# A fused attention and mixture kernel: the copy of the attention output one unit earlier, and the selection of the fourth query tile moved into the next batch

## What is computed

```python
att = where(causal, q @ k.T / sqrt(8), -inf)
S   = relu(att[:, 0]); S[..., 0] = 0; S = S * (1 - eye)      # head 0
FF  = cumsum(shift_down_by_one(S), axis=query)               # what is forgotten
att = att - FF
rank = argsort(argsort(where(causal, FF, inf)))
keep = (rank < minimum(102 - 1, i + 1)) | eye                # a fifth of the keys
y = softmax(where(keep, att, -inf)) @ v
x = x + y @ w_proj.T + b_proj + sum_e gate_e * (relu(inter_e) @ wo.T + bo)
```

## Time and profile before

| | |
|---|---|
| median of 3 runs | 747.84 us (745.73 to 748.78) |
| the profiled execution | 753.04 us, span 751.2 us |
| TensorE busy | 601.0 us (80% of the span) |
| VectorE busy | 538.1 us (72%) |
| ScalarE busy | 380.8 us (51%) |
| GpSimd busy | 437.9 us (58%) |
| mean granted clock of TensorE | 0.931 |

### The profile page before, as it was taken

One profiled execution on the slowest core, in us unless ns is written; L12 is line 12 of the kernel. 1 busy time (PEld: TensorE's weight loads), 2 busy tenths in 40 slices (PEclk: granted clock), 3 DMA queues, 4 the chain that ended last, 5 costly groups with the idle time before them and its releaser, 6 DMA issues. The chain is left out here.

```text
span 751.2 us, 16859 instructions
## 1 busy us (share of the span) xinstructions
PE 601.0 (80%) x5495; PEld 405.7 (54%) x5495; DVE 538.1 (72%) x2256; ACT 380.8 (51%) x813; POOL 437.9 (58%) x739
## 2 busy tenths in 40 slices
PE   4536798779887888779988888778887798779895
PEld 1314456556565656466565655556564564656474
DVE  7685648975599756995589856996479855985352
ACT  3444346445563555644564545645464555535542
POOL 6408455575736865376655856378554857348451
PEclk9866899899998899989998999999998999989998
DMA  4151620052001500034000520025000430000000
GB/s 88 19 58 20 67 23 16 1 68 33 1 16 29 64 8 1 16 49 52 1 15 12 63 28 2 15 37 63 3 1 2 59 41 1 2 12 5 2 1 15
DMA packets 27286, 18.98 MB, mean 25 GB/s; under 512 B 5417, under 2 KB 27072, under 8 KB 27200
## 3 DMA queue, kind: packets, MB, share of 16 engines
q1 hardware_dynamic: 27200, 17.91, 18.2%
HBM read 3.22 MB, written 2.10 MB: 7 GB/s over the span
## 5 line engine op out<-in xcount | busy, mean ns | idle before, releaser
L523 POOL TENSOR_SCALAR ar<-ar,mx 128x512 f32<-128x512 f32 (+3 forms) x512 | 282.1, 561 | 245.8 <-DVE mx L1221 244.5
L1221 DVE CUSTOM_DVE_ANT_0 ar<-ps_s,mask 128x512 f32<-128x512 f32 (+3 forms) x512 | 231.1, 484 | 52.1 <-PE ps_s L864 49.5
L877 PE MATMUL ps_t<-ident,ar 128*128 128x128 f32 x1280 | 212.2, 286 | 33.6 <-POOL ar L523 18.4
L690 ACT ACTIVATE pr<-ps_t 128x512 f32<-128x512 f32 (+1 forms) x352 | 190.9, 554 | 86.1 <-PE ps_t L877 85.1
L877 PEld LDWEIGHTS ps_t<-ident,ar 128*128 128x128 f32 x1280 | 160.4, 147 | 79.7 <-POOL ar L523 58.3
L864 PE MATMUL ps_s<-ks,qs 96*128 96x512 bf16 (+3 forms) x512 | 134.2, 315 | 31.0 <-DVE mx L1221 22.8
L896 PE MATMUL ps_o<-pr,va 128*32 128x128 f32 x2560 | 104.7, 295 | 27.3 <-ACT out_t L699 14.6
L896 PEld LDWEIGHTS ps_o<-pr,va 128*32 128x32 f32 x2560 | 67.3, 116 | 62.6 <-ACT pr L690 41.5
L675 ACT ACTIVATE h<-ps_m,bi_col 128x512 f32<-128x512 f32 x64 | 44.0, 687 | 101.5 <-PE ps_m L811 101.5
L864 PEld LDWEIGHTS ps_s<-ks,qs 96*128 96x128 bf16 x512 | 43.4, 100 | 80.8 <-DVE mx L1221 36.2
L811 PE MATMUL ps_m<-zm,b_t 128*128 128x512 f32 x128 | 66.9, 604 | 5.2 <-ACT h L675 5.2
(11 more groups left out here) (215 smaller groups left out, 780.2 us busy)
## 6 DMA issues: line engine op xcount, KB each, us to landing
qs<-parts SPq DMA_DIRECT2D x48, 128.0 KB
ks<-parts SPq DMA_DIRECT2D x48, 128.0 KB
xs<-in_L_attn_x SPq DMA_DIRECT2D x8, 256.0 KB, 3.0
out<-res SPq DMA_DIRECT2D x8, 192.0 KB, 2.0
out<-res SPq DMA_DIRECT2D x8, 64.0 KB, 6.4
ar<-in_L_ffn_wi SPq DMA_DIRECT2D x1, 256.0 KB, 3.3
ar<-in_L_ffn_wo SPq DMA_DIRECT2D x1, 256.0 KB, 3.9
ar<-in_L_ffn_lora_B SPq DMA_DIRECT2D x4, 64.0 KB, 4.1
```

The source lines that it names most:

```text
L523: nc.gpsimd.tensor_scalar(col, col, -1.0, mx[:, t % NA_RING, j:j + 1], ALU.mult, ALU.add)\
L690: nc.scalar.activation(pr[:, u % NP_RING, 0:w], ps_t[u % NT_RING][:, 0:w], ACT.Exp, scale=-1.0)\
L877: last = nc.tensor.transpose(ps_t[u % NT_RING][:, P * j:P * j + P], ar[:, u % NA_RING, P * j:P * j + P], ident[:, :])
L1221: nc.vector.tensor_tensor_reduce(out=ar[:, t % NA_RING, w * j:w * j + w], in0=ps_s[t % NS_RING][:, w * j:w * j + w], in1=mask[:, k % 2, OF ...
```

## The change

Three things are changed.

- `OUT_LAG` goes from 1 to 0. ScalarE's copy of `ps_o` now stands in the same step as the last value products of the tile, after that step's exponential; before, it stood one step later. It waits for the same semaphore.
- In the preparation of a batch the fourth tile (tile 3) is taken out of marks, top eights, replacements and mask. Its marks go to unit 12 of the batch itself, the first top eight and replacement to unit 13, the second to 14, the new step `last` to 15, its mask to 16. For tiles 0 to 2 the steps remain in units 34 to 40, but tile 2 becomes a group "middle" of its own: its first top eight is one unit later than before (36 for 35), its replacement 37 for 36, its second one at 38 and 40 for 38 and 39.
- The guard is split in two: tiles 0 to 2 at `flag`, as before, and tile 3 at `last`, which loads the same register and branches again. Each ends in a memset of the flag and adds one to `selected`, so ScalarE's waits count by two.

```diff
--- before.py
+++ after.py
@@ -66,7 +66,7 @@
 NBANKS = NM_RING + NT_RING + NS_RING + 1
 NA_RING, NP_RING = 7, 6
 LAG_T, LAG_P = 3, 4
-OUT_LAG, OT_LAG, YT_LAG = 1, 2, 4
+OUT_LAG, OT_LAG, YT_LAG = 0, 2, 4
 TAIL = 13
 
 QUAD = 4
@@ -94,10 +94,11 @@
     "f0": 9, "f1": 10, "f2": 11, "f3": 12,
     "gate": 14, "route": 16, "choices": 21, "share": 24,
     "search": 13,
-    "under_narrow": 21, "under_wide": 21, "reach": 21, "marks_narrow": 21, "marks_wide": 21,
-    "top0_narrow": 22, "top0_wide": 22, "replace0_narrow": 22, "replace0_wide": 22,
-    "top1_narrow": 22, "top1_wide": 22, "replace1_narrow": 22, "replace1_wide": 22,
-    "flag": 24, "mask_0": 24, "mask_1": 24, "mask_2": 24, "mask_3": 24, "v": 25,
+    "under": 21, "reach": 21, "marks_narrow": 21, "marks_middle": 21, "marks_wide": 12 + AHEAD,
+    "top0_narrow": 22, "top0_middle": 22, "replace0_narrow": 22, "replace0_middle": 22,
+    "top1_narrow": 22, "top1_middle": 22, "replace1_narrow": 22, "replace1_middle": 22,
+    "top0_wide": 13 + AHEAD, "replace0_wide": 13 + AHEAD, "top1_wide": 14 + AHEAD, "replace1_wide": 14 + AHEAD,
+    "flag": 24, "mask_0": 24, "mask_1": 24, "mask_2": 24, "v": 25, "last": 15 + AHEAD, "mask_3": 16 + AHEAD,
 }
 
 SECOND_AT = {
@@ -113,10 +114,11 @@
     "s0": 15, "s1": 16, "s2": 17, "s3": 18, "v": 16, "scan0": 16, "scan1": 17, "scan2": 18, "scan3": 19,
     "f0": 20, "f1": 21, "f2": 22, "f3": 23,
     "search": 24,
-    "under_narrow": 32, "under_wide": 32, "reach": 33, "marks_narrow": 34, "marks_wide": 34,
-    "top0_narrow": 35, "top0_wide": 35, "replace0_narrow": 36, "replace0_wide": 37,
-    "top1_narrow": 37, "top1_wide": 38, "replace1_narrow": 39, "replace1_wide": 40,
-    "flag": 41, "mask_0": 42, "mask_1": 45, "mask_2": 48, "mask_3": 50,
+    "under": 32, "reach": 33, "marks_narrow": 34, "marks_middle": 34, "marks_wide": 56,
+    "top0_narrow": 35, "top0_middle": 36, "replace0_narrow": 36, "replace0_middle": 37,
+    "top1_narrow": 37, "top1_middle": 38, "replace1_narrow": 39, "replace1_middle": 40,
+    "top0_wide": 57, "replace0_wide": 57, "top1_wide": 58, "replace1_wide": 58,
+    "flag": 41, "mask_0": 42, "mask_1": 45, "mask_2": 48, "last": 59, "mask_3": 60,
 }
 PREP_JOBS = [("xt", "act"), ("q", "act"), ("k", "act"), ("gate", "dve"), ("v", "dve")] + \
     [(f"s{c}", "act") for c in range(NA)] + [(f"f{a}", "dve") for a in range(NA)] + [("flag", "dve")]
@@ -604,7 +606,7 @@
                         for a in range(NA):
                             if t == at(f"mask_{a}", n):
 
-                                act.wait_ge(selected, n + 1)
+                                act.wait_ge(selected, 2 * n + (2 if a == NA - 1 else 1))
                                 data = work[:, a, PADS:PADS + P * (a + 1)]
                                 nc.scalar.activation(data, data, ACT.Relu, bias=half_mark[:, :])\
                                     .then_inc(limited, 1)
@@ -1119,25 +1121,29 @@
                         dve.wait_ge(dve_read, plan.reads["flag", n][1])
                         dve.wait_ge(dve_chain, chain[0])
                         link(nc.vector.tensor_copy(flag_i[:, :], flag[:, :]))
+                        again_from(0, NA - 1)
+
+                    def again_from(lo, hi):
+
                         failed = dve.value_load(flag_i[0:1, 0:1])
                         with dve.If(failed > 0):
                             dve.sem_clear(again)
-                            nc.vector.memset(work[:, :, 0:PADS], MARK).then_inc(again, 1)
+                            nc.vector.memset(work[:, lo:hi, 0:PADS], MARK).then_inc(again, 1)
                             dve.wait_ge(again, 1)
-                            nc.vector.memset(work[:, :, 0:8 * ROUNDS - KEEP], 1.0e37).then_inc(again, 1)
-                            for a in range(NA):
+                            nc.vector.memset(work[:, lo:hi, 0:8 * ROUNDS - KEEP], 1.0e37).then_inc(again, 1)
+                            for a in range(lo, hi):
                                 nc.vector.tensor_copy(work[:, a, PADS:PADS + P * (a + 1)], nf[:, OFF[a]:OFF[a + 1]])\
                                     .then_inc(again, 1)
-                            dve.wait_ge(again, 2 + NA)
+                            dve.wait_ge(again, 2 + hi - lo)
                             with dve.Fori(0, ROUNDS):
                                 dve.sem_clear(again)
-                                for a in range(NA):
+                                for a in range(lo, hi):
                                     nc.vector.max(top8[:, a, :], work[:, a, 0:PADS + P * (a + 1)]).then_inc(again, 1)
-                                for a in range(NA):
-                                    dve.wait_ge(again, a + 1)
+                                for a in range(lo, hi):
+                                    dve.wait_ge(again, a - lo + 1)
                                     row = work[:, a, 0:PADS + P * (a + 1)]
                                     nc.vector.match_replace(row, top8[:, a, :], row, MARK).then_inc(again, 1)
-                                dve.wait_ge(again, 2 * NA)
+                                dve.wait_ge(again, 2 * (hi - lo))
                         nc.vector.memset(flag[:, :], 0.0).then_inc(selected, 1)
 
                     nc.vector.memset(qs[:, 0].rearrange("p h t -> p (h t)").bitcast(F32), 0.0).then_inc(zeroed, 1)
@@ -1241,21 +1247,23 @@
                             r, odd = divmod(t - at("search", n), 2)
                             if 0 <= r < ROUNDS_IN:
                                 (search_step if odd else search_count)(n, r)
-                            for width, tiles in (("narrow", (0, 1, 2)), ("wide", (3,))):
-                                if t == at(f"under_{width}", n):
-                                    under_threshold(n, tiles)
+                            if t == at("under", n):
+                                under_threshold(n, range(NA))
                             if t == at("reach", n):
                                 in_reach()
-                            for width, tiles in (("narrow", (0, 1, 2)), ("wide", (3,))):
+                            for width, tiles in (("narrow", (0, 1)), ("middle", (2,)), ("wide", (3,))):
                                 if t == at(f"marks_{width}", n):
                                     marks(tiles)
                             for r in range(FAST):
-                                for width, tiles in (("narrow", (0, 1)), ("wide", (2, 3))):
+                                for width, tiles in (("narrow", (0, 1)), ("middle", (2,)), ("wide", (3,))):
                                     if t == at(f"top{r}_{width}", n):
                                         eight_largest(tiles)
-                                for width, tiles in (("narrow", (0, 1, 2)), ("wide", (3,))):
+                                for width, tiles in (("narrow", (0, 1)), ("middle", (2,)), ("wide", (3,))):
                                     if t == at(f"replace{r}_{width}", n):
                                         replace_largest(tiles)
+                            if t == at("last", n):
+                                dve.wait_ge(dve_chain, chain[0])
+                                again_from(NA - 1, NA)
 
             with nc.Block() as clear:
                 @clear.sync
```

## The result

| | before | after |
|---|---|---|
| median | 746.79 us (743.23 to 748.78, 4 runs) | 726.86 us (725.88 to 729.14, 4 runs) |
| ratio of after to before | | 0.970 (95%: 0.966 to 0.974) |
| profiled execution, span | 753.04 us, 751.2 us | 726.16 us, 724.4 us |
| mean granted clock of TensorE | 0.931 | 0.941 |

Faster, by 19.9 us between the medians, where 30.2 were forecast. Between the two profiled executions it is 26.9 us; the profiled execution of before was a long one (753.04 against a median of 746.79), that of after was not (726.16 against 726.86).

The account below looks back on a forecast made before the run. No engine was full on average; VectorE was taken to set the pace of units 28 to 43 and TensorE that of units 12 to 16. Savings of 19.8 + 10.4 = 30.2 us off 747.84 gave 717.6, range 701 to 733.

Parts of the forecast that it names:

- point 1: Units 34 to 40: the fourth tile's selection leaves VectorE, saving 2.7 us in six cycles and 3.6 in one, 19.8 us.
- point 4: Batch starts: the output copy one unit earlier shortens the value products' wait, 1.6 or 1.2 us a start, 10.4 us.
- rival A: Denser TensorE work keeps the 2.4 GHz clock at unit 38 and batch starts: 42.6 us saved, 705; chance 0.16.
- the floor of 1.96 a cycle: Units 34 to 40: least saving per cycle, only what reaches the transposes of unit 36, 1.96 us.
- the ceiling of 3.63: Units 34 to 40: most saving per cycle, all VectorE work removed, 3.63 us.
- Point 2: Units 12 to 15: the moved selection and second guard fit into 7.0 us of VectorE idle time; cost nothing.
- the forecast's own sign of being wrong: Wrong if the stretch of units 12 to 19 grows by over 0.5 us.
- Point 3: Units 6 to 16: moving the fourth mask costs nothing, but narrowly, with 2.2 us of cover; bound 0.5 a batch.
- Point 5: Start and end: first scores waited for the stacks' DMA, last chain already has copy behind products; nothing gained.
- B: Units 34 to 40 and batch starts: TensorE takes over, saving only 18.9 us, giving 729; chance 0.19.
- C: VectorE's saved time turns into waits or the edit shortens nothing: within 0.5%, 748; chance 0.05.
- D: Unit 16: a pile-up of mask 3, shift, diagonals and `hsum` on GpSimd costs 37.6 us, giving 755; chance 0.06.

Follow-up runs that it names:

- before_later: The kernel before with the second and third parts of q and k one unit later and nothing else: 748.10 us, ratio 0.997.
- no_wide: The changed kernel without the fourth tile's marks, top eights and replacement: 729.57 us in one run.
- after_again: The changed kernel once more, timed on one chip with move_again: 726.48 us, ratio 0.969 to the kernel before.
- move_again: The changed kernel with the output copy back at its old unit (same kernel as move_only), on one chip with after_again: 726.28 us, ratio 0.970.
- copy_only: The kernel before with the output copy one unit earlier and nothing else: 741.03 us, ratio 0.990.
- move_only: The changed kernel with the output copy back at its old unit: 726.80 us, ratio 0.971 to the kernel before.
- later_fill: split_later with the four score fills from the stacks and their scans one unit later, the value product one unit earlier: 712.44 us, ratio 0.946.
- split_later: The changed kernel with the second and third parts of q and k one unit later: 721.03 us, ratio 0.964 to the kernel before.
- four_parts: The changed kernel with four transfers a stack instead of six, the two smallest partial products left out of the scores: 714.87 us, ratio 0.956.

## Why the prediction was right or wrong

The sign and the range held, and the likeliest value missed by 9 us: the sum came to 30.2, measured were 19.9 between medians, or 26.6 between the profiled executions counted from the first mask addition. Two thirds of the miss lie in how the sum was put on the median. It was made against the profiled execution and taken off a median 5.2 us lower, "profiling or chance". The record speaks for chance: the profiled execution of after lies 0.7 us below its median, and those of the later runs from 3.6 us below to 3.8 above theirs. Against the profiled run the forecast was 722.8, and 726.16 came. The rest is a balance of errors: point 1 gave 6.3 less, units 12 to 16 took 2.9, and units 4 to 11 gave 4.1 more than point 4, through falls of the clock that the sum left out and rival A had.

**Point 1 (19.8).** The mechanism was right: before_later shows VectorE bounding units 34 to 40, and the selection's leaving shortens them and nothing else does. The size, 2.7 a cycle, was wrong. In after it came to 13.5 us, the floor of 1.96 a cycle. With the move alone it is 17.4 to 20.0 us, 3.3 to 3.5 in the batches whose clock stays full: near the ceiling of 3.63 that was set aside. The step that failed is "Then TensorE has its own 6.9 us of work, which VectorE's further savings don't shorten". Rows 2 showed 6.8 us of that work at half clock, and before took the same 15.44 us in batch 1 with 0.8 at half clock. At full clock all of units 34 to 40 takes 12.15 us with VectorE 11.3 busy, so "what is late next is VectorE still" holds there. In after the clock fell in each of the seven cycles, and TensorE at half clock came next. The exponential behind the part of q adds a gap ahead of the fall, but at full clock the gap costs nothing.

**Point 2 (0).** Right for the moved work: VectorE 8.84 us busy in the stretch (9.5 forecast), and no_wide gets nothing back. But the stretch grew all the same in batches 3, 5 and 6, and this was the forecast's own sign of being wrong. The step that is missing is in point 4: what TensorE meets when it comes 2.7 us earlier to unit 15. The transfers of the stacks weren't looked at outside the start (rows 9), though they span 26.7 to 28.4 us in batches 1 to 6 of before, with 0.8 to 4.0 of slack.

**Point 3 (0).** Right, and as narrow as said. In after:

```profile
350.67 1.22 POOL L525 TENSOR_SCALAR ar<-ar,mx 128x384 f32<-128x384 f32 x1
...
352.64 0.49 PE L879 MATMUL ps_t<-ident,ar 128*128 128x128 f32 x3
```

The shift of unit 17 ends at 351.89, 0.75 us ahead of its transposes, for 2.2 in before (rows 7), and they don't wait.

**Point 4 (10.4).** The term was right to 0.5 us: after_again is 10.1 below move_again in units 4 to 11 (1.4 of it a fall of the clock in batch 5 of move_again), and in the last batch units 28 to 33 give 0.8 more. What failed is the word "sum". With what units 12 to 16 (2.9) and 34 to 40 (7.4) give back it is worth nothing beside the move (726.48 and 726.28), 11 alone in the trace and 7.8 between medians (copy_only, rest 689.6 to 678.5), and 11 to 14 when the wait for the stacks is mended and the falls are fewer or cheaper. The added wait at the copy was harmless, as argued.

**Point 5 (0).** Right to 0.2 us in the profiled pair (61.62 and 61.45).

**The rivals.** A (the clock follows) is what move_only did in batches 1 to 3, with no fall at unit 36 or at the batch start. In after it came halfway, from 105 to 88 us at half clock. B gave nearly the measured time (729), half by its own mechanism: point 1 came at its floor, as B has it, though for TensorE at half clock and not for its work as such. Point 4, which B halves, was whole, and other stretches took it back; that the times agree is luck. C and D didn't happen.

## What to carry to other kernels

When an edit makes one stage shorter, list everything on its own clock that later stages meet (transfers with their end and their slack, not only waits that exist already): a slack of 2.8 us was invisible in the table of waits, and using it up took back some 2 us. Measure two edits of one change apart and together before adding their prices, since here 11 and 23 to 25 us made 25 to 27 in the traces. And after a bound is lifted, read the queue of each other engine at that place for an instruction that waits with ready work behind it; giving it one more unit of time gave 6 to 7 us here. Then look at what the wait costs at each level of the clock, since the same edit gave 0.2 to 2.4 us with the copy late. And don't take the distance between one profiled execution and the median for a constant: the 5.2 us here did not come back.

## What the runs showed of the hardware

**The clock falls behind the same gap in one kernel and not in another.** Two traces with equal work and equal idle time in the 3.4 us before (1.51 us busy) went on at 1.2 and at 2.4 GHz; in the 3.3 us ahead of those TensorE was busy 2.18 and 2.81 us. What decides was not tried separately and stays open. In units 34 to 40 the five runs with the selection moved, the copy early and the parts of q in their old place have a fall in all seven cycles, move_only in four and move_again in three, though these two are one kernel.

**The price of a fall depends on where it lies.** One of 3.4 us costs 1.2 to 1.5 us in units 34 to 40 of after and after_again in batches 1, 2, 3 and 5 (13.4 to 13.6 for 12.15), 0.7 in later_fill (12.82), 0.6 in units 17 to 27 (23.51 for 22.92 in split_later), and nothing in units 0 to 3 (6.45 either way in after) or in before's units 34 to 40, where VectorE sets the pace.

**The stacks' transfers take their time whatever the batch does.** Twelve of 128 KB take 25.5 to 28.5 us from issue to the last packet in batches 1 to 6 of every kernel that has twelve, at a DMA share of 0.55 and 66 GB/s, other transfers included, over the 27.6 us of batch 3 of after, and shortening every batch around them changes nothing in that. Eight take 20.1 to 20.7 (four_parts).

**Batch 4 takes longer than its neighbours in units 12 to 16**, by 1.4 us in before (13.73 for 12.34) and by 1.8 in later_fill (13.36 for 11.59), but not in four_parts (12.35). It went with two of six transfers fewer, so it hangs on the stacks' traffic too; through which instruction, no run shows.
